# Third layer's attention of a decoder: norms by powers block by block, and its output by batches

## The chip, the cores and the metric

The kernel runs on one core of one Trainium2 chip. A core has five engines, each with an instruction stream of its own: TensorE (PE, matrix products), VectorE (DVE), ScalarE (ACT), GpSimd (POOL) and SyncE (SP), which here only issues DMAs. They wait for each other through semaphores. Transfers run on 16 DMA engines, fed through queues that belong to the issuing engine. The metric is the device time of one execution in microseconds (us). The kernel before takes 1616.43 us, the median of three runs (1613.71 to 1619.91).

## What is computed

A decoder of four layers, each with an attention, a cross attention and a feed-forward part, over 4 batches of 256 tokens with 256 features, in float32. The change touches the attention of the third layer (the code counts from 0 and calls it `l2a_`):

```python
def _softmax_kernel(x, R):
    n = jnp.sqrt(jnp.sum(x * x, axis=-1, keepdims=True))
    x = x / jnp.maximum(n, 1e-06)
    p = jnp.einsum('...d,ed->...e', x, R)
    feats = jnp.concatenate([jnp.sin(p), jnp.cos(p)], axis=-1)
    return feats / math.sqrt(F)
q = (hidden_states @ Wq.T + bq).reshape(b, s, H, D).transpose(0, 2, 1, 3)
k = (hidden_states @ Wk.T + bk).reshape(b, s, HKV, D).transpose(0, 2, 1, 3)
v = (hidden_states @ Wv.T + bv).reshape(b, s, HKV, D).transpose(0, 2, 1, 3)
q = q * cos + _rotate_half(q) * sin
k = k * cos + _rotate_half(k) * sin
k = jnp.repeat(k, rep, axis=1)
v = jnp.repeat(v, rep, axis=1)
qp = _softmax_kernel(q, rand_matrix)
kp = _softmax_kernel(k, rand_matrix)
kv = jnp.einsum('bhsf,bhsd->bsfd', kp, v)
out = jnp.einsum('bhsf,bsfd->bhsd', qp, kv)
out = out.reshape(b, s, HID)
return out @ Wo.T + bo
```

There are 16 query heads and 8 heads of keys and values, of 16 features each. Features are sine and cosine of a random projection of the normalised vector, and the sum over heads is taken for each token by itself. The final reshape goes from (batch, head, token, feature) straight to (batch, row, 256), so it mixes heads and tokens. The input of the stage is a layer norm of the residual, and its output is added to the residual.

## The kernel before

Stages of the decoder run one after the other; every stage is a block of code for each engine, and the next one starts when all engines have ended. `feature_attention` is the stage of the change. Rows of features stand on 128 partitions, the 1024 tokens along the free axis. Keys and values fill one such block (`k0`, `v`), queries two (`q0`, `q1`).

PSUM is used as four pairs of banks of 1024 columns. `Jobs` gives each product in turn the next pair; a list made at the start names the jobs in order and who empties each. `wait_room` makes TensorE wait until the job four places ahead has been emptied, `wait_filled` makes the taker wait for the product.

The front. TensorE projects k, q0, q1, each in two jobs (straight, and with swapped halves for the rotation; the latter's name ends in `s`), then v. VectorE takes each pair of jobs with `rotate` (two operations with cos and sin, one sum) and squares the result. TensorE then forms the squared norms of all three blocks (24 products with 8 columns, `norm`) and the projections by the random matrix (`pk0`, `pq0`, `pq1`). ScalarE takes the root of all norms at once (192 columns), VectorE clamps, inverts and scales them, and makes the turns of each block: product by the inverse norm, a quarter turn for the cosines, and taking away the whole turns. ScalarE applies the sine, TensorE transposes the features back (`fk0`, `fq0`, `fq1`), and ScalarE copies them into `keys` and `q_rows`.

SyncE then makes seven rotated copies each of keys and values, each by two DMAs that shift them by whole heads over the partitions (`rotate_heads`): values first, for all tokens, then keys by halves of the tokens.

The steps. For each half of the tokens there are 8 steps, one for each rotation. VectorE multiplies queries by keys (`by_heads`), TensorE sums over a head's features with a matrix of ones (`weigh`), VectorE multiplies the weights by the values (`mix`), GpSimd adds the results of two steps, and TensorE adds them up in PSUM by transposing them (`add`). The code is written so that `by_heads` of the next step comes before `mix`.

The tail. For each half, ScalarE copies the sums to `att`, SyncE stores four tiles in a scratch of device memory in the order (batch, head, token, feature) and loads them back by rows, TensorE transposes them (`turn_rows`), ScalarE copies, TensorE multiplies by the output matrix (`project_out`) and VectorE adds to the residual. The order of all this is the order in which the code is written for each engine; no scheduler changes it. The layer norm's own inverse root is already made by powers on GpSimd, on 4 columns at a time (`norm_gpsimd`, line 166):

```python
nc.gpsimd.tensor_tensor(m.rstd[:, 1, tiles], m.rstd[:, 0, tiles], m.minus_half[:, tiles], ALU.pow)
```

`m.minus_half` is a small tensor filled with -0.5. In the listing below, lines 2098 to 2100 are the list of jobs, 2133 to 2152 SyncE, 2157 to 2160 GpSimd, 2163 to 2242 TensorE, 2247 to 2273 ScalarE and 2278 to 2339 VectorE.

## Time and profile before

| | |
|---|---|
| median of the runs | 1616.43 us (1613.71 to 1619.91) |
| the profiled execution | 1623.54 us, of which span 1621.7 us |
| busy share of the span: TensorE, VectorE, ScalarE, GpSimd | 70%, 65%, 30%, 35% |
| DMA over the span | 195.87 MB, mean 121 GB/s |
| this stage: first projection to last addition to the residual | 883.16 to 1007.98 us |

The shares are averages over twelve stages with different limits, so they say little on one of them. In the rows, times are counted from the span's start; a row of a timeline may stand for several instructions of one kind, and what stands in brackets is the idle time of the engine before them and what ended it. One product in float32 leaves two records on TensorE, so a job of four 512-column products counts as 8. The granted clock is given in parts of the full 2.4 GHz; 0.50 is the lower of its two levels, 1.2 GHz.

### The profile page before, as it was taken

What the parts mean: (1) busy time and instruction counts of PE and PEld (TensorE: products, weight loads), DVE (VectorE), ACT (ScalarE), POOL (GpSimd) and SP (SyncE); (2) the same over time, 40 slices, a digit from 0 to 9 for tenths busy, and PEclk for the clock granted to TensorE, in tenths of its full rate; (3) what the DMA queues carried; (4) which work ended last, traced back from release to release, by engine and by line L of the source; (5) the groups of instructions that cost most, each with busy time, mean ns of one, the idle gap of its engine ahead of it and who ended that gap; (6) DMA issues with size and microseconds to landing.
All of it is one profiled execution on the core that took longest, in us unless ns stands there. A gap on an engine that the chain in (4) does not pass through costs nothing. (4 is left out here: it accounts for less than half of the span.)

```text
span 1621.7 us, 21361 instructions
## 1 busy us (share of the span) xinstructions
PE 1140.4 (70%) x6058; PEld 718.6 (44%) x6058; DVE 1059.8 (65%) x1790; ACT 492.7 (30%) x949; POOL 575.6 (35%) x596
## 2 busy tenths in 40 slices
PE   7445547999309695554998896699847878866970
PEld 3211235777004572122565644577634324445860
DVE  6999975773695557998885683320345878745454
ACT  3423322333402252332211200343313346622430
POOL 0046613552755113662000042023440632204746
PEclk9769987999659898998999888799978859987985
DMA  5074347996321403433300432142520140048944
GB/s 189 31 255 148 114 137 225 306 315 228 95 68 33 125 4 130 155 130 133 117 1 0 120 77 37 43 144 77 173 85 7 30 129 3 3 125 249 329 137 123
DMA packets 138562, 195.87 MB, mean 121 GB/s; under 512 B 35408, under 2 KB 98914, under 8 KB 137196
## 3 DMA queue, kind: packets, MB, share of 16 engines
q1 hardware_dynamic: 104316, 145.85, 29.0%
q0 software_dynamic: 12704, 29.36, 6.3%
q10 hardware_dynamic: 21456, 19.60, 3.9%
q8 instruction: 43, 0.70, 0.2%
q14 instruction: 43, 0.35, 0.1%
HBM read 142.80 MB, written 31.72 MB: 108 GB/s over the span
## 5 line engine op out<-in xcount | busy, mean ns | idle before, releaser
L165 POOL TENSOR_SCALAR rstd<-moments 128x4 f32<-128x4 f32 x24 | 6.5, 270 | 410.1 <-DVE moments L148 410.1
L177 PE MATMUL psum<-w_ident,h 128*128 128x128 f32 x144 | 29.8, 389 | 110.6 <-DVE h L155 110.6
L558 PE MATMUL psum<-l1s_read,w_ident 128*128 128x512 f32 x128 | 64.9, 630 | 53.5 <-DVE l1s_read L623 53.4
L558 PE MATMUL psum<-l0s_read,w_ident 128*128 128x512 f32 x128 | 65.4, 636 | 52.2 <-DVE l0s_read L623 52.2
L1906 DVE TENSOR_REDUCE l3x_neg<-psum 128x2 f32<-128x512 f32 x128 | 80.7, 683 | 23.9 <-PE psum L1777 23.9
L1881 ACT ACTIVATE l3x_work<-psum 128x512 f32<-128x512 f32 x128 | 72.5, 598 | 50.9 <-PE psum L1800 50.6
L546 POOL TENSOR_TENSOR l1s_drive<-l1s_du,l1s_bc 128x1024 f32<-128x1024 f32 x32 | 75.3, 2355 | 35.3 <-DVE psum L619 35.3
L546 POOL TENSOR_TENSOR l0s_drive<-l0s_du,l0s_bc 128x1024 f32<-128x1024 f32 x32 | 75.2, 2353 | 35.3 <-DVE psum L619 35.3
L177 PEld LDWEIGHTS psum<-w_ident,h 128*128 128x128 f32 x144 | 25.4, 202 | 117.6 <-DVE h L155 115.3
L1162 PE MATMUL psum<-l0f_w_in,l0f_xT 128*128 (+1 forms) x224 | 76.8, 466 | 0.0
L1037 POOL DMA_INDIRECT l3f_x<-l3f_h_rows,l3f_token_of x64 | 59.3, 927 | 48.5 <-DVE l3f_token_of L1433 28.5
L1028 POOL DMA_INDIRECT l0f_x<-l0f_h_rows,l0f_token_now x56 | 59.0, 1053 | 46.6 <-PE psum L1152 18.2
L619 DVE TENSOR_TENSOR_SCAN psum<-psum,l1s_drive 128x1024 f32<-128x1024 f32 x32 | 73.2, 2287 | 0.0
L619 DVE TENSOR_TENSOR_SCAN psum<-psum,l0s_drive 128x1024 f32<-128x1024 f32 x32 | 73.2, 2286 | 0.0
L189 ACT ACTIVATE hT<-psum 128x512 f32<-128x512 f32 x36 | 19.4, 595 | 159.6 <-PE psum L177 159.5
L558 PEld LDWEIGHTS psum<-l1s_read,w_ident 128*128 128x128 f32 x128 | 22.2, 193 | 96.2 <-DVE l1s_read L623 80.3
L558 PEld LDWEIGHTS psum<-l0s_read,w_ident 128*128 128x128 f32 x128 | 22.4, 195 | 95.2 <-DVE l0s_read L623 79.1
L595 ACT ACTIVATE psum<-late,w_l1s_a 128x1024 f32<-128x1024 f32 x32 | 35.7, 1118 | 80.0 <-DVE l1s_read L623 79.4
L595 ACT ACTIVATE psum<-l0s_delta,w_l0s_a 128x1024 f32<-128x1024 f32 x32 | 35.7, 1118 | 80.0 <-DVE l0s_read L623 79.4
L1192 PE MATMUL psum<-l3f_xT,l3f_w_in 128*96 128x96 f32 x528 | 58.0, 255 | 0.3 <-ACT l3f_xT L1293 0.3
L1181 PE MATMUL psum<-l0f_w_down,l0f_gatedT 88*128 (+1 forms) x224 | 57.6, 380 | 0.0
L1192 PEld LDWEIGHTS psum<-l3f_xT,l3f_w_in 128*96 128x96 f32 x528 | 52.3, 171 | 0.6 <-issue 0.5
(642 smaller groups left out, 3131.1 us busy)
## 6 DMA issues: line engine op xcount, KB each, us to landing
l0f_w_in<-in_l0f_w_in SPq DMA_DIRECT2D x56, 352.0 KB
l0s_bc<-l0s_scratch SPq DMA_DIRECT2D x16, 1024.0 KB, 5.1
l1s_bc<-l1s_scratch SPq DMA_DIRECT2D x16, 1024.0 KB, 5.2
l3f_w_in<-in_l3f_w_in SPq DMA_DIRECT2D x32, 384.0 KB
l0f_w_down<-in_l0f_w_down SPq DMA_DIRECT2D x56, 176.0 KB
l2f_w_in<-in_l2f_w_in SPq DMA_DIRECT2D x24, 352.0 KB
l0f_y_rows<-l0f_y ACTq DMA_DIRECT2D x56, 128.0 KB
l3f_w_down<-in_l3f_w_down SPq DMA_DIRECT2D x32, 192.0 KB
```

Of the source, the lines that this page charges most:

```text
L177: ins = nc.tensor.transpose(m.psum[:, at:at + P], m.h[:, t, k * P:(k + 1) * P], m.ident[:])
L546: nc.gpsimd.tensor_tensor(drive[c], du[:, c, :], bc[s][:, 0, :], ALU.mult).then_inc(drive_ready, 1)
L558: ins = nc.tensor.matmul(m.pair(2 + c)[:, cols], lhsT=m.ident[:], rhs=rhs[:, cols], start=start, stop=stop, skip_group_check=True)
L595: nc.scalar.activation(decay[c], delta[:, c, :], ACT.Exp, scale=w["a"][:, c, bass.ds(at, 1)]).then_inc(decay_ready, 1)
L619: nc.vector.tensor_tensor_scan(state[c], decay[c], drive[c], 0.0, ALU.mult, ALU.add).then_inc(scanned, 1)
L1028: nc.gpsimd.indirect_dma_start(x[s][:], None, h_rows, bass.IndirectOffsetOnAxis(ap=token_now[s // 2][:, s % 2:s % 2 + 1], axis=0)).then_in ...
L1037: nc.gpsimd.indirect_dma_start(x[b % ROWS][0:L, :], None, h_rows, bass.IndirectOffsetOnAxis(ap=token_of[0:L, b:b + 1], axis=0)).then_inc(x ...
L1162: ins = nc.tensor.matmul(in_ps[d % 2], lhsT=xT[d % 2][:, k, :], rhs=w, start=(k == 0), stop=(k == KD - 1))
L1181: ins = nc.tensor.matmul(y_ps[d % 2], lhsT=gatedT[d % 2][:, c, :], rhs=w, start=(c == 0), stop=(c == chunks - 1))
L1192: ins = nc.tensor.matmul(feature_ps[i][:, f, :], lhsT=w_in[:, at, k, f * F:(f + 1) * F], rhs=xT[i][:, k, 0:L], start=(k == 0), stop=(k == ...
L1881: nc.scalar.activation(self.prob[i % 8][:, 0:self.keys], self.bank(3 + i % 3)[:, 0:self.keys], ACT.Exp).then_inc(self.exp_done, 1)
L1906: ins = nc.vector.tensor_reduce(self.neg[k % 2][:, :, hl], bank[:, 0:self.keys].rearrange("p (q k) -> p q k", q=self.maxima), AX_X, ALU.ma ...
```

## The change

The norm is now made for each block by itself, as soon as that block is squared. The squared norms of one block are a job of its own (64 columns), emptied by VectorE, which clamps them at 1e-12; GpSimd raises them to the power -0.5 and so gives the inverse norm; VectorE applies it with the factor of the turns in one operation. The square root on ScalarE, the reciprocal and the two scalings are gone. The order on TensorE, VectorE and ScalarE is rewritten so that norms and turns of one block stand between the projections of others. Keys are copied before values, both by halves of the tokens, and each rotation of the values has its own semaphore.

In the tail, work goes by batch in place of halves of the tokens. Sums of a batch are announced as soon as its two tiles are added; stores and loads of batches 0 and 2 go through SyncE's queue, those of 1 and 3 through ScalarE's. Semaphores count accordingly.

```diff
-    jobs = Jobs(m, tag + "in", 2, [(f"{x}{c}{s}", "vector") for x, c in chunks for s in ("", "s")]
-                + [("v", "scalar"), ("norm", "scalar")] + [(f"p{x}{c}", "vector") for x, c in chunks]
-                + [(f"f{x}{c}", "scalar") for x, c in chunks])
+    takers = dict(n="vector", p="vector", f="scalar")
+    order = ["k0", "k0s", "q0", "q0s", "nk0", "pk0", "q1", "q1s", "nq0", "pq0", "fk0", "nq1", "pq1", "v", "fq0", "fq1"]
+    jobs = Jobs(m, tag + "in", 2, [(x, "scalar" if x == "v" else takers.get(x[0], "vector")) for x in order])
...
+
+    def rows_out(eng, b):
+        eng.wait_ge(att_done, b + 1)
+        for t in range(2 * b, 2 * b + 2):
+            dst = scratch[b, :, t % 2 * P:(t % 2 + 1) * P, :].rearrange("h s d -> s h d")
+            eng.dma_start(dst, att[:, t, :].rearrange("p (h d) -> p h d", d=HD)).then_inc(stored[b], 16)
+
+    def rows_back(eng, b):
+        eng.wait_ge(stored[b], 32)
+        eng.dma_start(m.h[:, 2 * b:2 * b + 2, :], by_rows[b]).then_inc(att_back[b], 16)
...
-            sp.wait_ge(jobs.empty("v"), 1)
-            for r in range(1, ROUNDS):
-                rotate_heads(sp, values, r, slice(0, T), values_in)
-            sp.wait_ge(jobs.empty("fk0"), 3)
             for h in range(2):
+                for rows, made, done in ((keys, jobs.empty("fk0"), keys_in), (values, jobs.empty("v"), values_in)):
+                    if h == 0:
+                        sp.wait_ge(made, 1 if rows is keys else 2)
+                    for r in range(1, ROUNDS):
+                        if h:
+                            sp.wait_ge(done[r], 32)
+                        rotate_heads(sp, rows, r, halves[h], done[r])
+            for b in (0, 2):
+                rows_out(sp, b)
+                rows_back(sp, b)
...
+            for i in range(len(chunks)):
+                pool.wait_ge(norm_ready, i + 1)
+                nc.gpsimd.tensor_tensor(norm[:, i, :], norm[:, i, :], m.minus_half[:, 0:1].to_broadcast([P, TILES * HPC]),
+                                        ALU.pow).then_inc(powered, 1)
...
+                for name, lhs, rhs in ((f"n{k}{c}", sq[f"{k}{c}"], w("same")[:, 0:P:HD]), (f"p{k}{c}", x[f"{k}{c}"], w("rand")[:])):
+                    jobs.wait_room(pe, name)
+                    n = rhs.shape[1]
+                    for t in range(TILES):
+                        ins = nc.tensor.matmul(jobs.pair(name)[:, t * n:(t + 1) * n], lhsT=lhs[:, t * P:(t + 1) * P],
+                                               rhs=rhs, start=True, stop=True)
...
+            project_chunk(0)
+            project_chunk(1)
+            norm_and_turns(0)
+            project_chunk(2)
+            norm_and_turns(1)
+            turn_feats(0)
+            norm_and_turns(2)
+            project(m, pe, jobs, "v", wcols(w("v"), 0), hT, KD)
+            turn_feats(1)
+            turn_feats(2)
...
+                    if t % 2:
+                        ins.then_inc(added, 1)
...
+            for h in range(2):
+                for b in (2 * h, 2 * h + 1):
+                    turn_rows(b)
+                if h == 0:
+                    pe.wait_ge(mix_done, STEPS)
+                for b in (2 * h, 2 * h + 1):
+                    project_out(b)
...
+            sine(0)
+            take_feats(0)
+            sine(1)
             jobs.wait_filled(act, "v")
             nc.scalar.activation(values[:, 0, :], jobs.pair("v"), ACT.Identity, bias=w("v_b")[:, 0:1]).then_inc(jobs.empty("v"), 1)
-            jobs.wait_filled(act, "norm")
-            nc.scalar.activation(norm[:].rearrange("p a t h -> p (a t h)"),
+            sine(2)
+            take_feats(1)
+            take_feats(2)
+
+            def take_sums(b):
+                act.wait_ge(added, 2 * (b // 2 + 1) * STEPS // 4 - (1 - b % 2))
...
             take_sums(0)
             take_sums(1)
+            rows_out(act, 1)
+            rows_back(act, 1)
+            take_sums(2)
+            take_sums(3)
+            rows_out(act, 3)
             take_rows(0)
             take_rows(1)
+            rows_back(act, 3)
+            take_rows(2)
+            take_rows(3)
 
...
+            def take_norm(i):
+                k, c = chunks[i]
+                name = f"n{k}{c}"
+                jobs.wait_filled(dve, name)
+                nc.vector.tensor_scalar(norm[:, i, :], jobs.pair(name)[:, 0:TILES * HPC], 1e-12, None, ALU.max).then_inc(norm_ready, 1)
+                dve.wait_ge(norm_ready, i + 1)
+                dve.sem_inc(jobs.empty(name), 1)
+
+            def turns(i, meanwhile=None):
+                k, c = chunks[i]
                 name = f"p{k}{c}"
                 jobs.wait_filled(dve, name)
+                dve.wait_ge(powered, i + 1)
+                r = norm[:, i, :].unsqueeze(2).to_broadcast([P, TILES * HPC, HD])
+                nc.vector.scalar_tensor_tensor(out=heads(f), in0=heads(jobs.pair(name)), scalar=float(1 / TWO_PI), in1=r, op0=ALU.mult,
+                                               op1=ALU.mult).then_inc(jobs.empty(name), 1)
...
+            turn_chunk(0)
+            turn_chunk(1)
+            take_norm(0)
+            turns(0)
+            turn_chunk(2)
+            take_norm(1)
+            o.link(dve, nc.vector.tensor_tensor(m.resid[:], m.resid[:], w("o_b")[:].unsqueeze(1).to_broadcast([P, TILES, D]),
+                                                ALU.add))
+            turns(1, lambda: take_norm(2))
+            turns(2)
...
+            for b in range(B):
+                dve.wait_ge(out_filled, b + 1)
+                r = m.resid[:, 2 * b:2 * b + 2, :]
+                nc.vector.tensor_tensor(r, bank(4 + b).rearrange("p (t d) -> p t d", d=D), r, ALU.add).then_inc(out_added, 1)
+            dve.wait_ge(out_added, B)
```

Three places where instructions move. In the names, `sq` is first the square and then the turns and features of a block, `w_l2a_same` the matrix of ones, `w_l2a_rand` the random matrix; `w_ident` marks transpositions.

TensorE, from the first projection to the last transposition of features, before:

```order
L239 MATMUL psum<-hT,w_l2a_k 128x512 x8
L239 MATMUL psum<-hT,w_l2a_q 128x512 x16
L239 MATMUL psum<-hT,w_l2a_v 128x512 x4
L2178 MATMUL psum<-w_l2a_same,l2a_sq_k 128x8 x8
L2178 MATMUL psum<-w_l2a_same,l2a_sq_q 128x8 x16
L2185 MATMUL psum<-w_l2a_rand,l2a_k 128x128 x8
L2185 MATMUL psum<-w_l2a_rand,l2a_q_rows 128x128 x16
L2193 MATMUL psum<-w_ident,l2a_sq_k 128x128 x8
L2193 MATMUL psum<-w_ident,l2a_sq_q 128x128 x16
```

and now:

```order
L239 MATMUL psum<-hT,w_l2a_k 128x512 x8
L239 MATMUL psum<-hT,w_l2a_q 128x512 x8
L2189 MATMUL psum<-w_l2a_same,l2a_sq_k 128x8 x8
L2189 MATMUL psum<-w_l2a_rand,l2a_k 128x128 x8
L239 MATMUL psum<-hT,w_l2a_q 128x512 x8
L2189 MATMUL psum<-w_l2a_same,l2a_sq_q 128x8 x8
L2189 MATMUL psum<-w_l2a_rand,l2a_q_rows 128x128 x8
L2199 MATMUL psum<-w_ident,l2a_sq_k 128x128 x8
L2189 MATMUL psum<-w_l2a_same,l2a_sq_q 128x8 x8
L2189 MATMUL psum<-w_l2a_rand,l2a_q_rows 128x128 x8
L239 MATMUL psum<-hT,w_l2a_v 128x512 x4
L2199 MATMUL psum<-w_ident,l2a_sq_q 128x128 x16
```

The second q block's projections now stand behind the norms and turns of k, and the values' projection behind all norms; two of the three 8-column groups stand between products of 128 or 512 columns.

VectorE, from the second block's square on, before:

```order
L2287 TENSOR_TENSOR l2a_sq_q<-l2a_q_rows 128x1024
L1556 SCALAR_TENSOR_TENSOR l2a_rot<-psum,w_l2a_q_b,w_l2a_cos 128x1024
L1556 SCALAR_TENSOR_TENSOR l2a_rot<-psum,w_l2a_q_b,w_l2a_sin 128x1024
L1559 TENSOR_TENSOR l2a_q_rows<-l2a_rot 128x1024
L2287 TENSOR_TENSOR l2a_sq_q<-l2a_q_rows 128x1024
L2289 TENSOR_TENSOR resid<-resid,w_l2a_o_b 128x2048
L2293 TENSOR_SCALAR l2a_norm<-l2a_norm 128x192
L2294 RECIPROCAL l2a_norm<-l2a_norm 128x192
L2295 TENSOR_SCALAR l2a_norm<-l2a_norm 128x192
L2302 TENSOR_TENSOR l2a_sq_k<-psum,l2a_norm 128x1024
L2305 TENSOR_SCALAR l2a_sq_k<-l2a_sq_k 128x64x8
L2306 TENSOR_SCALAR l2a_whole<-l2a_sq_k 128x1024
```

and now:

```order
L2324 TENSOR_TENSOR l2a_sq_q<-l2a_q_rows 128x1024
L2330 TENSOR_SCALAR l2a_norm<-psum 128x64
L2342 SCALAR_TENSOR_TENSOR l2a_sq_k<-psum,l2a_norm 128x1024
L2347 TENSOR_SCALAR l2a_sq_k<-l2a_sq_k 128x64x8
L2348 TENSOR_SCALAR l2a_whole<-l2a_sq_k 128x1024
L2349 TENSOR_TENSOR l2a_sq_k<-l2a_sq_k,l2a_whole 128x1024
L1556 SCALAR_TENSOR_TENSOR l2a_rot<-psum,w_l2a_q_b,w_l2a_cos 128x1024
L1556 SCALAR_TENSOR_TENSOR l2a_rot<-psum,w_l2a_q_b,w_l2a_sin 128x1024
L1559 TENSOR_TENSOR l2a_q_rows<-l2a_rot 128x1024
L2324 TENSOR_TENSOR l2a_sq_q<-l2a_q_rows 128x1024
L2330 TENSOR_SCALAR l2a_norm<-psum 128x64
L2358 TENSOR_TENSOR resid<-resid,w_l2a_o_b 128x2048
```

The turns of k stand ahead of the second q block's rotation and behind a clamp and a power; the addition of the bias stands between a clamp and the multiplication that needs its power.

ScalarE, end of the front and the tail, before (it issues no DMA there):

```order
L2258 ACTIVATE l2a_q_rows<-psum 128x1024
L2256 ACTIVATE l2a_sq_q<-l2a_sq_q 128x1024
L2258 ACTIVATE l2a_q_rows<-psum 128x1024
L2262 ACTIVATE l2a_att<-psum 128x1024 x2
L2267 ACTIVATE hT<-psum 128x2x512 x2
```

and now:

```order
L2272 ACTIVATE l2a_sq_q<-l2a_sq_q 128x1024
L2277 ACTIVATE l2a_q_rows<-psum 128x1024 x2
L2290 ACTIVATE l2a_att<-psum 128x512 x2
L2138 DMA l2a_scratch<-l2a_att 128x16x16 x2
L2142 DMA h<-l2a_scratch 128x2x256
L2290 ACTIVATE l2a_att<-psum 128x512 x2
L2138 DMA l2a_scratch<-l2a_att 128x16x16 x2
L2295 ACTIVATE hT<-psum 128x2x256 x2
L2142 DMA h<-l2a_scratch 128x2x256
L2295 ACTIVATE hT<-psum 128x2x256 x2
```

The values' copy, now in front of the last sine, is above the first of these rows. Between the copies of sums and of rows, ScalarE now issues the stores and loads of two batches, and waits for each store before its load.

## Rows read from the trace of the kernel before

**Rows 1.** Timeline of PE, projections: start us, busy us, engine, line, operation.

```profile
890.03 13.90 PE L239 MATMUL psum<-hT,w_l2a_q 128*128 128x512 f32 x32
```

**Rows 2.** Windows: stretch, length, busy us of each engine, PEclk, DMA share, GB/s.

```profile
907.00:934.00 27.00, 20.48 (x121) 19.14 (x119) 15.89 (x18) 10.19 (x10) 0.00 (x0) 0.69 0.72 191
...
944.00:986.00 42.00, 39.55 (x187) 24.46 (x188) 33.35 (x27) 1.53 (x2) 24.25 (x8) 1.00 0.23 30
986.00:1008.30 22.30, 12.49 (x43) 9.55 (x41) 2.45 (x2) 2.45 (x3) 0.00 (x0) 0.77 0.38 47
```

**Rows 3.** Timeline of DVE, front.

```profile
899.75 1.23 DVE L2287 TENSOR_TENSOR l2a_sq_q<-l2a_q_rows 128x1024 f32<-128x1024 f32 x1
900.89 1.28 DVE L1556 SCALAR_TENSOR_TENSOR l2a_rot<-psum,w_l2a_q_b,w_l2a_cos 128x1024 f32<-128x1024 f32 x1
...
907.76 2.28 DVE L2289 TENSOR_TENSOR resid<-resid,w_l2a_o_b 128x2048 f32<-128x2048 f32 x1
915.06 0.26 DVE L2293 TENSOR_SCALAR l2a_norm<-l2a_norm 128x192 f32<-128x192 f32 x1 [5.02 <-ACT l2a_norm L2252]
...
918.31 1.23 DVE L2302 TENSOR_TENSOR l2a_sq_k<-psum,l2a_norm 128x1024 f32<-128x1024 f32 x1 [1.31 <-PE psum L2185]
...
928.17 1.23 DVE L2307 TENSOR_TENSOR l2a_sq_q<-l2a_sq_q,l2a_whole 128x1024 f32<-128x1024 f32 x1
933.74 1.23 DVE L2316 TENSOR_TENSOR l2a_prod<-l2a_q_rows,l2a_keys 128x1024 f32<-128x1024 f32 x1 [4.34 <-ACT l2a_q_rows L2258]
```

**Rows 4.** Timeline of PE, front: norms, turns, transposition.

```profile
907.20 1.85 PE L2178 MATMUL psum<-w_l2a_same,l2a_sq_k 128*128 128x8 f32 x16
...
914.44 3.76 PE L2185 MATMUL psum<-w_l2a_rand,l2a_k 128*128 128x128 f32 x16
917.99 4.97 PE L2185 MATMUL psum<-w_l2a_rand,l2a_q_rows 128*128 128x128 f32 x32
923.22 1.06 PE L2193 MATMUL psum<-w_ident,l2a_sq_k 128*128 128x128 f32 x8 [0.26 <-ACT l2a_sq_k L2256]
```

**Rows 5.** Groups of POOL by form: busy us, mean ns, idle before.

```profile
L546 POOL TENSOR_TENSOR l1s_drive<-l1s_du,l1s_bc 128x1024 f32<-128x1024 f32 x32 | 75.3, 2355 | 35.3 <-DVE psum L619 35.3
...
L166 POOL TENSOR_TENSOR rstd<-rstd,minus_half 128x4 f32<-128x4 f32 x24 | 25.0, 1043 | 2.0
...
L1738 POOL TENSOR_TENSOR l3x_neg_rest<-l3x_neg,l3x_neg_parts 128x16 f32<-128x16 f32 x16 | 3.5, 216 | 1.4
```

**Rows 6.** Instructions on the tile of keys: min/median/max ns, first and last start.

```profile
L2129 SPq DMA_DIRECT2D l2a_keys<-l2a_keys x14: 589/594/611, 925.9 to 942.5; - x14
...
DMA to landing us min/median/max: 2.1/2.4/2.9
```

**Rows 7.** Timeline of PE, begin of the steps.

```profile
935.11 8.34 PE L2201 MATMUL psum<-l2a_prod,w_l2a_same 128*128 128x512 f32 x12 [2.54 <-DVE l2a_prod L2316]
...
948.27 3.60 PE L2201 MATMUL psum<-l2a_prod,w_l2a_same 128*128 128x512 f32 x8
```

**Rows 8.** Timeline of the SP queue, second half's stores and loads.

```profile
986.54 4.03 SPq L2149 DMA_DIRECT2D l2a_scratch<-l2a_att  x4
991.46 3.23 SPq L2152 DMA_DIRECT2D h<-l2a_scratch  x2
```

**Rows 9.** Waits of the SP queue between 994.2 and 996 us.

```profile
SPq L2152 <- DMA l2a_scratch<-l2a_att: 2.2, 1, 2.2
```

**Rows 10.** Timeline of PE, tail.

```profile
987.57 3.69 PE L2228 MATMUL psum<-w_l2a_o,hT 128*128 128x256 f32 x16 [1.25 <-ACT hT L2267]
997.13 1.94 PE L2220 MATMUL psum<-w_ident,h 128*128 128x128 f32 x8 [5.86 <-DMA h<-l2a_scratch]
1000.18 6.53 PE L2228 MATMUL psum<-w_l2a_o,hT 128*128 128x256 f32 x16 [1.11 <-ACT hT L2267]
```

**Rows 11.** Timeline of ACT and of DVE, tail.

```profile
985.49 1.03 ACT L2262 ACTIVATE l2a_att<-psum 128x1024 f32<-128x1024 f32 x1 [19.32 <-PE psum L2210]
...
1006.75 1.23 DVE L2338 TENSOR_TENSOR resid<-psum,resid 128x1024 f32<-128x1024 f32 x1 [14.22 <-PE psum L2228]
```

More of the change, by code:

```diff
@@ L2218, in turn_rows @@
+                                               start=(first == 0 and c == 0 and t % 2 == 0), stop=(first == STEPS // 4 - 1),
+                                               skip_group_check=True)
+                    if t % 2:
+                        ins.then_inc(added, 1)
+            def turn_rows(b):
+                pe.wait_ge(att_back[b], 16)
                 for c in range(KD):
-                    for t in range(4):
-                        ins = nc.tensor.transpose(m.pair(h)[:, c * HALF + t * P:c * HALF + (t + 1) * P],
-                                                  m.h[:, 4 * h + t, c * P:(c + 1) * P], m.ident[:])
+                    for t in range(2):
+                        ins = nc.tensor.transpose(bank(b)[:, c * S + t * P:c * S + (t + 1) * P],
+                                                  m.h[:, 2 * b + t, c * P:(c + 1) * P], m.ident[:])
@@ L2222, in turn_rows, with project_out @@
                 ins.then_inc(rows_turned, 1)
-            def project_out(h):
-                pe.wait_ge(hT_done, h + 1)
-                for t in range(4):
+            def project_out(b):
+                pe.wait_ge(hT_done, b + 1)
+                for t in range(2):
+                    at = (2 * b + t) * P
                     for k in range(KD):
-                        ins = nc.tensor.matmul(m.pair(2 + h)[:, t * D:(t + 1) * D], lhsT=m.hT[:, k, (4 * h + t) * P:(4 * h + t + 1) * P],
+                        ins = nc.tensor.matmul(bank(4 + b)[:, t * D:(t + 1) * D], lhsT=m.hT[:, k, at:at + P],
@@ L2229, in project_out @@
                                                rhs=w("o")[:, k, :], start=(k == 0), stop=(k == KD - 1))
                 ins.then_inc(out_filled, 1)
-            for name in ("fq0", "fq1"):
-                pe.wait_ge(jobs.empty(name), jobs.takers[:jobs.at(name) + 1].count("scalar"))
+            pe.wait_ge(jobs.empty("fq1"), 4)
             for s in range(STEPS):
@@ L2248, in _, with sine, take_feats @@
             m.wait_weights(act, tag)
+            def sine(i):
+                k, c = chunks[i]
+                act.wait_ge(turns_ready, i + 1)
+                nc.scalar.activation(sq[f"{k}{c}"][:], sq[f"{k}{c}"][:], ACT.Sin, scale=SIN_SCALE).then_inc(feats_ready, 1)
+            def take_feats(i):
+                k, c = chunks[i]
+                jobs.wait_filled(act, f"f{k}{c}")
+                nc.scalar.activation(turned_to[f"{k}{c}"], jobs.pair(f"f{k}{c}"), ACT.Copy).then_inc(jobs.empty(f"f{k}{c}"), 1)
@@ L2334, in _ @@
                 mix(s)
-            for h in range(2):
-                dve.wait_ge(out_filled, h + 1)
-                r = m.resid[:, 4 * h:4 * h + 4, :]
-                nc.vector.tensor_tensor(r, m.pair(2 + h).rearrange("p (t d) -> p t d", d=D), r, ALU.add).then_inc(out_added, 1)
-            dve.wait_ge(out_added, 2)
+            for b in range(B):
[3 more added lines that the diff above has]
+            dve.wait_ge(out_added, B)
 def context_mixing(m, n, j):
```

100 lines of the change are left out of this document (27 added, 73 removed).

## Prediction

> **What bounds the kernel now.** I read the page's forty slices to find the third layer's attention, then the windows over its stretch, then the timelines of VectorE, TensorE, ScalarE and the SyncE queue inside it. The stage ends at 1008 us and has a front, sixteen steps and a tail. Up to 907 the projections keep TensorE busy without a gap: 32 matmul records of 512 columns take 13.90 us, so 3.5 us for one job of 8 [rows 1]. From 907 to 934 lies the part of the front that the change rearranges, and nothing is full there: in 27 us TensorE works 20.5, VectorE 15.9, ScalarE 10.2, at a mean granted clock of 0.69 [rows 2]. Then come the steps; in 944 to 986 TensorE is busy 39.6 of 42 us, so they are TensorE's, and the change leaves their instructions as they are [rows 2]. In the tail, 986 to 1008.3, TensorE works 12.5 us and VectorE 2.45 [rows 2]; it waits for round trips through device memory.
>
> In the front VectorE adds the bias from 907.76 on and then waits 5.02 us until 915.06 for one ScalarE square root, behind which all 24 norm groups of TensorE stand. Two more waits follow, 1.31 us before the first multiplication by the norm and 4.34 us before the first step, which starts at 933.74 [rows 3].
>
> **The front after the change.** I walk it from 900.98, where the second square ends (899.75 + 1.23) [rows 3]; up to there all engines have the same work in the same order.
>
> TensorE's own chain, at the full granted clock: a group of norms of 8 columns takes 1.85 us, one of 128 columns 4.97 / 2 = 2.49, a projection job 3.5, a transposition of features 1.06 [rows 1, 4]. The first q block ends at 897.1. Behind it end the norm at 899.0, the turns 901.4, the second q block 908.4, its predecessor's norm 910.3, turns 912.8, features of k 913.9, last norm 915.8, turns 918.3, values 921.8. This chain needs VectorE in time.
>
> The power is the unknown. The trace has powers on 4 columns only, 1043 ns each; an ordinary two-input operation on 16 columns takes 216 ns, on 1024 columns 2355, so 2.1 ns for a column [rows 5]. The new power has 64 columns and is there three times. Lower end: the whole surplus is a fixed cost, 1.04 + 60 x 0.0021 = 1.2 us. Upper end: the surplus of 1.043 - 0.216 = 0.83 us belongs to the 4 columns, 0.207 us each, and 64 x 0.207 + 0.3 = 13.5 us. No row lies between; the only row of a power is sixteen times smaller. I take the geometric mean of the two ends, 4.0 us, and carry both.
>
> With 4.0 us: the clamp of the norm (0.26 us, as at 915.06 for 192 columns) ends at 901.2, its power at 905.2. The turns of one block took 3.7 us (three from 918.31 to 929.40) [rows 3]: k's end at 908.9. The rotation and square of the second q block are two operations of 1.28 and two of 1.23 us, with gaps 5.1: 914.0. Clamp 914.3, power 918.3; the bias add of 2.28 us lies beside it, 1.7 us stay bare. The first multiplication of q0 ends at 919.6, the third clamp at 919.9, its power at 923.9; the other 2.4 us of q0's turns lie beside it, 1.6 us stay bare. Turns of q1: 927.7. From there to the first step come sine, transposition and copy, 4.34 us as now [rows 3]: 932.0. The front wins 1.7 us. Behind VectorE's wait on the first power stands the second q block's rotation, and behind that its norm and turns on TensorE; so each us of power above 4 counts three times. At 1.2 us the walk ends at 927.1, 6.6 us won (then TensorE's 921.8 and the copy of the values in front of the last sine are what is late); at 13.5 us it ends at 960.3, 26.5 lost.
>
> Costed at nothing: the square root and three small VectorE operations leave, but what counts is when the first multiplication starts, and that is in the walk. The two table loads lay in ScalarE's waits. Keys leave earlier, but did not bind: the first step waited for ScalarE [rows 3]. Values now leave behind the keys' first half. 28 copies of keys are issued in 17.1 us, one every 0.63, and land 2.4 us later [rows 6]; so keys go from 915.1 to 924.0 and values to 933.3, the first landing near 928, asked for near 938. Without that cover the price would be the lateness of one pair, under 2 us. The steps run as now with their slow begin, where 12 matmul records take 8.34 us and 8 take 3.60 later [rows 7]. If TensorE's clock stayed up, because its gap before the first step is shorter, 8.3 - 5.4 = 3 us more would be won; I count nothing.
>
> **The tail.** Now the last addition ends at 985.45 and the copy of both batches at 986.5. Four stores are issued from 986.54 to 990.57, the first load at 991.46, the second behind a wait of 2.2 us, its issue ending at 994.69; TensorE starts at 997.13 [rows 8 to 11]. Then 1.94 us of transpositions, a copy, 6.53 us of output matmuls and 1.23 us of VectorE, to 1008.0. The matmuls ran at the lower clock; the first half's took 3.69 us [rows 10].
>
> After the change the additions of batch 2 end 1.0 us before those of batch 3 (half a group, 8 records of 128 columns, 1.06 us [rows 4]) and its copy has half the size, so its stores go at 985.1, those of batch 3 at 986.2 on ScalarE's queue. Bounds: if the queues really ran side by side, the last store would land 4.9 us after its queue's start (991.46 - 986.54), at 991.1, and TensorE could take batch 3 some 2.8 us later, at 993.9, 3.2 us earlier than now. If the DMA engines are the limit, only the earlier start counts, 1.4 us. I take 2.1: 995.0. Then transpositions of half the size (0.5 or 1.0 us), two output groups of half the size (3.69 or 6.53 us together) and an add of 0.65 us, with batch 3's copy beside batch 2's matmuls: 999.9 at the full clock, 1003.2 at half. TensorE's gap before is shorter, since the output of batches 0 and 1 now waits for ScalarE's store issues and ends near 992.4. I take the middle, 1001.5: 6.5 us won (3 to 9 by these bounds).
>
> The Trainium skill, DMA: Bandwidth & Descriptors, section Issuing engines are not separate DMA queues, says that issuing on several engines saves only the sequencer's time. By it the stores end with the engines' work, and the tail would win 5.8 us in place of 6.5. No row of this trace has two queues storing at once.
>
> **Sum.** The profiled execution took 1623.54 us (span 1621.7), 7 us above the median of 1616.43. -1.7 - 6.5 = -8.2: 1615 for a profiled execution, 1608 for the median.
>
> **Rivals.**
> A, the forecast: the power costs between 1.2 and about 5.5 us. The walk gives -6.6 to +2.8 for the front, the tail -6.5: 1603 to 1613, with the tail's own bounds and the clock at the begin of the steps 1599 to 1614. Chance 0.50.
>
> B, slower: the power's cost lies in its columns, 13.5 us. Place: VectorE's wait in front of the second q block, and again before q0's and q1's turns. +26.5 - 6.5 = +20: 1636. Below 4.0 + 8.2 / 3 = 6.7 us for a power the tail pays for the front; from there on it decides. For it: 0.83 us is much for a mere start. Against it: small ordinary operations on GpSimd pay almost only a start [rows 5]. Chance 0.26.
>
> The Trainium skill, GPSIMD Engine Reference, section Instruction dispatch, puts the dispatch of an instruction at tens of cycles and all else into a loop over the elements. That rule makes B right; the trace, with powers of one size alone, cannot say.
>
> C: a power of 5.5 to 9.5 us: -3.7 to +8 in all, 1613 to 1624. Chance 0.12.
>
> D: TensorE's clock falls in the front, since 8-column groups now stand between dense ones. The trace has it at its lower level behind them: 16 records of 128 columns took 3.76 us in place of 2.49, 1.5 times [rows 4]. From the second norm to the values TensorE has 9.8 us of such groups, which become 14.7 by that factor, and 3.5 us of projection, which would double to 7: 8.4 us more. Values 930, the first step near 936, 2 us later than now: 1616.4 + 2 - 6.5 = 1612. Against it: each 8-column group is now only 1.85 us long. Chance 0.06.
>
> E: two queues and smaller pieces win nothing but the earlier start, at the lower clock: -1.7 - 4 = 1611. Chance 0.06.
>
> **How the numbers follow.** Faster or slower means by over 0.5%, 8.1 us, about what a measurement of this kernel can tell from no change. A gives 0.46 faster and 0.04 the same, B 0.26 slower, C 0.10 the same and 0.02 slower, D and E 0.02 faster together (with a power near the lower end) and 0.10 the same: faster 0.48, same 0.24, slower 0.28. Cases of both signs hold weight, so the range takes in B: 1599 to 1637. The forecast's own is 1599 to 1614.
>
> **What would show it.** The three powers of 64 columns on GpSimd: near 4 us each confirms the walk; 1 us puts the first step near 927, 13 us near 960. VectorE's waits in front of the three multiplications by the norm should read 4.0, 1.7 and 1.6 us. TensorE's output matmuls of batches 2 and 3, 3.7 or 6.5 us together, and its start on batch 3's rows, 9.5 us after the last addition in place of 11.7, show the tail. The walk is wrong in itself if a step waits for values or keys, if the second q block does not follow the first turns without a gap on TensorE, or if first step to last addition, 51.7 us now, changes by more than the 3 us of its slow begin.

## The result, and the profile after

| | before | after |
|---|---|---|
| median of the runs, us | 1616.58 | 1634.18 |
| lowest to highest, us | 1613.71 to 1619.91 | 1631.12 to 1637.93 |
| profiled execution, us (span) | 1623.54 (1621.7) | 1632.96 (1631.1) |

The change makes the kernel slower: ratio 1.0101, interval 1.0073 to 1.0128, where 1608 us, a gain, were forecast; 1634 lies inside the wide range of 1599 to 1637, on the side of rival B. The time lies in the three powers. They took 10.52 us each, not 4.0. GpSimd's timeline after (start us, busy us, engine, line, operation, idle before) answers to [rows 5], where powers have 4 columns:

```profile
896.17 10.52 POOL L2164 TENSOR_TENSOR l2a_norm<-l2a_norm,minus_half 128x64 f32<-128x64 f32 x1 [20.17 <-DVE l2a_norm L2330]
915.84 10.52 POOL L2164 TENSOR_TENSOR l2a_norm<-l2a_norm,minus_half 128x64 f32<-128x64 f32 x1 [9.16 <-DVE l2a_norm L2330]
928.06 10.52 POOL L2164 TENSOR_TENSOR l2a_norm<-l2a_norm,minus_half 128x64 f32<-128x64 f32 x1 [1.70 <-DVE l2a_norm L2330]
```

VectorE's timeline of the front, for [rows 3]. The second square ends at 894.73 + 1.22 = 895.95:

```profile
894.73 1.22 DVE L2324 TENSOR_TENSOR l2a_sq_q<-l2a_q_rows 128x1024 f32<-128x1024 f32 x1
895.87 0.22 DVE L2330 TENSOR_SCALAR l2a_norm<-psum 128x64 f32<-128x64 f32 x1
906.80 1.23 DVE L2342 SCALAR_TENSOR_TENSOR l2a_sq_k<-psum,l2a_norm 128x1024 f32<-128x1024 f32 x1 [10.71 <-POOL l2a_norm L2164]
...
915.92 2.36 DVE L2358 TENSOR_TENSOR resid<-resid,w_l2a_o_b 128x2048 f32<-128x2048 f32 x1 [0.16 <-DVE l2a_norm L2330]
926.50 1.23 DVE L2342 SCALAR_TENSOR_TENSOR l2a_sq_q<-psum,l2a_norm 128x1024 f32<-128x1024 f32 x1 [8.22 <-POOL l2a_norm L2164]
...
938.72 1.23 DVE L2342 SCALAR_TENSOR_TENSOR l2a_sq_q<-psum,l2a_norm 128x1024 f32<-128x1024 f32 x1 [8.10 <-POOL l2a_norm L2164]
...
946.73 2.36 DVE L2369 TENSOR_TENSOR l2a_prod<-l2a_q_rows,l2a_keys 128x1024 f32<-128x1024 f32 x2 [4.33 <-ACT l2a_q_rows L2277]
```

Read it as a chain. Each multiplication by the norm (L2342) waits for its own power, and the next power can't start before VectorE has come on: the powers begin at 896.17, 915.84 and 928.06, none beside another. The waits are 10.71, 8.22 and 8.10 us. The sine, transposition and copy before the first step are as before, 4.33 us against 4.34 [rows 3].

TensorE in the front, for [rows 4] (the last row begins the steps, as in [rows 7]):

```profile
894.78 0.83 PE L2189 MATMUL psum<-w_l2a_rand,l2a_k 128*128 128x128 f32 x6
895.45 7.03 PE L239 MATMUL psum<-hT,w_l2a_q 128*128 128x512 f32 x16
902.32 1.85 PE L2189 MATMUL psum<-w_l2a_same,l2a_sq_q 128*128 128x8 f32 x16
908.08 3.78 PE L2189 MATMUL psum<-w_l2a_rand,l2a_q_rows 128*128 128x128 f32 x16 [3.91 <-DVE l2a_sq_k L2342]
...
927.78 6.05 PE L239 MATMUL psum<-hT,w_l2a_v 128*128 128x512 f32 x8 [5.12 <-DVE l2a_sq_q L2342]
...
948.10 8.19 PE L2218 MATMUL psum<-l2a_prod,w_l2a_same 128*128 128x512 f32 x12 [2.53 <-DVE l2a_prod L2369]
```

The first row is the end of the turns of k, since the view begins at 895; the second q block (895.45) follows it without a gap. Then TensorE waits twice for a multiplication that stands behind a power (3.91 and 5.12 us), and the values' 8 records take 6.05 us at a mean granted clock of 0.61, where such a job took 3.5 before [rows 1]. Neither sets the end: VectorE asks for nothing of theirs before its own third power is ready.

The windows cut the stage at the second square's end, the first step, the last addition's end and the last residual addition's end, for [rows 2]:

```profile
895.95:946.73 50.78, 29.00 (x112) 20.64 (x110) 18.66 (x22) 7.24 (x7) 31.55 (x3) 0.73 0.27 79
946.73:997.95 51.22, 47.11 (x194) 26.97 (x195) 40.31 (x32) 1.79 (x3) 25.18 (x8) 0.94 0.40 87
997.95:1013.82 15.87, 12.16 (x48) 9.60 (x46) 2.76 (x4) 2.77 (x5) 0.00 (x0) 0.78 0.54 66
```

Before, the same stretches took 32.8 (900.98 to 933.74 [rows 3]), 51.7 and 22.5 us (985.45 to 1007.98 [rows 11]). So +18.0 in the front, -0.5 in the steps, -6.7 in the tail: +10.8 between these points. In the first window GpSimd's 31.55 us are the powers alone.

The tail after: TensorE (for [rows 10]), then SyncE's queue and ScalarE's (for [rows 8, 9]):

```profile
997.78 1.04 PE L2238 MATMUL psum<-w_ident,h 128*128 128x128 f32 x8
1001.56 6.69 PE L2247 MATMUL psum<-w_l2a_o,hT 128*128 128x256 f32 x16 [2.73 <-ACT hT L2295]
1008.09 1.04 PE L2238 MATMUL psum<-w_ident,h 128*128 128x128 f32 x8
1009.37 3.72 PE L2247 MATMUL psum<-w_l2a_o,hT 128*128 128x256 f32 x16 [0.25 <-ACT hT L2295]
```

```profile
997.71 1.30 SPq L2138 DMA_DIRECT2D l2a_scratch<-l2a_att  x2
1003.93 0.36 SPq L2142 DMA_DIRECT2D h<-l2a_scratch  x1
```

```profile
998.61 2.16 ACTq L2138 DMA_DIRECT2D l2a_scratch<-l2a_att  x2
1000.82 1.08 ACT L2295 ACTIVATE hT<-psum 128x512 f32<-128x512 f32 x2 [2.23 <-issue]
1005.21 0.37 ACTq L2142 DMA_DIRECT2D h<-l2a_scratch  x1
```

From the first store to the start of the last load's issue pass 7.5 us (997.71 to 1005.21). On one queue it was some 7.8: the first store at 986.54, the last load's issue over at 994.69 [rows 8, 9], and one such issue takes 0.36 us. Two queues made the stores hardly faster. TensorE takes up the rows of batches 2 and 3 at 1008.09, 10.1 us after the last addition; before it was 11.7, and 9.5 were forecast. But the output of these batches now follows at once on that of batches 0 and 1 and runs at the full granted clock, 1.00 in place of 0.56: 3.72 us for 6.53 [rows 10]. The other output paid for it: 6.69 us at 0.55 in place of 3.69. It lies beside the round trip, where it costs little: with one queue the last rows were taken up 2.6 us after their load's issue began, which gives 1007.8 here as an estimate, against 1008.09.

### The profile page after: what moved, and what is told of

The parts are those of the page before. It is cut to its first block and busy times, and to the rows that moved or that the text cites. A ratio compares the mean times of both kernels' runs of the same rounds, so it can differ in the third digit from the quotient of the medians.

```text
span 1631.1 us, 21386 instructions
## 1 busy us (share of the span) xinstructions
PE 1140.8 (70%) x6057; PEld 723.9 (44%) x6058; DVE 1059.5 (65%) x1792; ACT 490.3 (30%) x950; POOL 605.4 (37%) x599
## 5 line engine op out<-in xcount | busy, mean ns | idle before, releaser
L546 POOL TENSOR_TENSOR l1s_drive<-l1s_du,l1s_bc 128x1024 f32<-128x1024 f32 x32 | 75.2, 2352 | 35.3 <-DVE psum L619 35.3
L546 POOL TENSOR_TENSOR l0s_drive<-l0s_du,l0s_bc 128x1024 f32<-128x1024 f32 x32 | 75.2, 2352 | 35.3 <-DVE psum L619 35.3
L1881 ACT ACTIVATE l3x_work<-psum 128x512 f32<-128x512 f32 x128 | 72.7, 599 | 50.8 <-PE psum L1800 50.4
L1037 POOL DMA_INDIRECT l3f_x<-l3f_h_rows,l3f_token_of x64 | 59.3, 926 | 50.8 <-DVE l3f_token_of L1433 28.7
L1028 POOL DMA_INDIRECT l0f_x<-l0f_h_rows,l0f_token_now x56 | 58.7, 1049 | 47.0 <-POOL l0f_token_now L1020 17.9
```

The source lines that it names most:

```text
L546: nc.gpsimd.tensor_tensor(drive[c], du[:, c, :], bc[s][:, 0, :], ALU.mult).then_inc(drive_ready, 1)
L1028: nc.gpsimd.indirect_dma_start(x[s][:], None, h_rows, bass.IndirectOffsetOnAxis(ap=token_now[s // 2][:, s % 2:s % 2 + 1], axis=0)).then_in ...
L1037: nc.gpsimd.indirect_dma_start(x[b % ROWS][0:L, :], None, h_rows, bass.IndirectOffsetOnAxis(ap=token_of[0:L, b:b + 1], axis=0)).then_inc(x ...
L1881: nc.scalar.activation(self.prob[i % 8][:, 0:self.keys], self.bank(3 + i % 3)[:, 0:self.keys], ACT.Exp).then_inc(self.exp_done, 1)
```

## The experiments

Theory: the three powers of 10.5 us stand one after another on the path to the first step, and each us of a power counts three times; the tail gives 6 to 7 us back. "Stage" below is the time in a profile from the start of the first power of the layer norm ahead of the attention to that of the next layer norm: 132.8 and 130.4 us in two profiles of before, 143.6 after. The brackets behind a ratio are its 95% interval, the ratio is to the kernel before timed beside it (median 1618 to 1621 us), and a difference in us without a further word is the ratio's.

**The change again.**

> The changed kernel once more, with more rounds. The profile of this stage accounts for 10.9 us of loss (18.0 in the front, -0.5 in the steps, -6.7 in the tail), the timed runs said 17 with an interval from 12 to 21. Theory (the stage is all): 1627 to 1629, ratio 1.007. Rival (something of the change costs 5 us more elsewhere): 1633 or more.

1635.0 us, ratio 1.0103 [1.0080, 1.0127], stage 143.8 and 1487.4 outside it. The slowdown repeats, and the number is the rival's, not the theory's. The stage accounts for 11 to 13 of about 17 us. Outside the stage the profiles of all kernels here lie between 1482.4 and 1492.9 us with no order that I can see, before itself at 1482.4 and 1488.9. So some 3 to 6 us of the slowdown stay unassigned. All other kernels below with the changed order of the front, but the one with half a power, are likewise timed 1 to 6 us slower than their stage says. Whether this is real is not shown.

**Each half alone.** The kernel before with the new output by batches, and the changed front with the old output. Of the first, SyncE's part (the second has the reverse, against the kernel after):

```diff
-            for h in range(2):
-                sp.wait_ge(att_done, h + 1)
...
+            for b in (0, 2):
+                rows_out(sp, b)
+                rows_back(sp, b)
```

> The kernel before with the new tail alone (output by batches, two queues). My theory: the slower time comes from the three powers of the front, and the tail wins. By the trace of the changed kernel the tail from the last addition to the last residual addition is 15.9 us against 22.5, so this kernel is 6.7 us faster than before: 1610. Rival 1 (the tail's gain is given back in the stages behind, or the two queues disturb others): no change, within 2 us. Rival 2 (the tail itself costs): slower.

1612.19 us, ratio 0.9958 [0.9943, 0.9974], -6.8 us, as expected: this half is a gain. From the last addition to the last residual addition pass 15.1 us.

> The changed front (norms by powers, new order, keys before values) with the tail of before. Theory: the front lost 18.0 us from the second square to the first step, all of it in three waits for powers of 10.5 us, so 1616.6 + 17.5 = 1634. Rival (half of the lost time is not in this stage): less than 1628 here, and the rest would show with the changed kernel.

1641.78 us, 1.0151 [1.0131, 1.0171], +24.4; the stage took 151.2, +18.4 to +20.8. Direction right, 7 us more than expected; again some us are outside the stage. The two halves add up: +24.4 - 6.8 = +17.6, against +16.7 for the whole.

**No power.** GpSimd multiplies in place of raising to the power:

```diff
-                                        ALU.pow).then_inc(powered, 1)
+                                        ALU.mult).then_inc(powered, 1)
```

> The changed kernel with a multiplication by -0.5 in place of each power, on the same 64 columns (the features then come from wrongly scaled vectors; all else is the same). Theory: the length of the power is the whole loss. A two-input operation on 64 columns takes about 0.3 us, so VectorE's walk ends about 5 to 6 us ahead of before, the tail wins 6.7, in all 1603 to 1605, with the clock perhaps 3 us more at the begin of the steps. Rival (the new order itself costs: TensorE's low clock behind the 8-column groups, values issued late): 1612 or more.

1605.32 us, 0.9924 [0.9907, 0.9941], some 29 us under after and just above the 1603 to 1605 expected. 26.6 us of the 29 are in the stage (117.1 us). GpSimd, then VectorE with its second rotation, q0's multiplication by the norm and the first step:

```profile
897.08 0.29 POOL L2164 TENSOR_TENSOR l2a_norm<-l2a_norm,minus_half 128x64 f32<-128x64 f32 x1 [20.96 <-DVE l2a_norm L2330]
...
903.50 1.28 DVE L1556 SCALAR_TENSOR_TENSOR l2a_rot<-psum,w_l2a_q_b,w_l2a_sin 128x1024 f32<-128x1024 f32 x1 [1.03 <-PE psum L239]
...
909.99 1.23 DVE L2342 SCALAR_TENSOR_TENSOR l2a_sq_q<-psum,l2a_norm 128x1024 f32<-128x1024 f32 x1
...
921.28 2.36 DVE L2369 TENSOR_TENSOR l2a_prod<-l2a_q_rows,l2a_keys 128x1024 f32<-128x1024 f32 x2 [3.46 <-ACT l2a_q_rows L2277]
```

The second square ends at 896.86 there, so the front takes 24.4 us in place of 32.8. The order of the change is a gain of 8.4 us there; the power alone turns it over. (This kernel leaves the inverse root out and is otherwise the changed one.)

**Half a power.** The power covers 32 of 64 columns:

```diff
-                nc.gpsimd.tensor_tensor(norm[:, i, :], norm[:, i, :], m.minus_half[:, 0:1].to_broadcast([P, TILES * HPC]),
+                nc.gpsimd.tensor_tensor(norm[:, i, 0:32], norm[:, i, 0:32], m.minus_half[:, 0:1].to_broadcast([P, 32]),
```

> The changed kernel with each power on 32 of its 64 columns only (the other norms stay squared; all else is the same). Theory: 0.41 + 32 x 0.158 = 5.5 us for a power, 5.05 less, and all three waits are still bare, so 15 us less than the changed kernel: ratio near 1.001, 1620. Rival (the loss above 4 us does not count three times, because other chains then bind): 1625 or more.

1617.69 us, 0.9981 [0.9961, 1.0001], 2 to 3 us under the expectation.

```profile
902.06 5.42 POOL L2164 TENSOR_TENSOR l2a_norm<-l2a_norm,minus_half 128x32 f32<-128x32 f32 x1 [20.95 <-DVE l2a_norm L2330]
...
937.31 2.36 DVE L2369 TENSOR_TENSOR l2a_prod<-l2a_q_rows,l2a_keys 128x1024 f32<-128x1024 f32 x2 [4.33 <-ACT l2a_q_rows L2277]
```

From 901.85 to 937.31 are 35.5 us. With after's 50.8 the slope is (50.8 - 35.5) / (10.52 - 5.42) = 3.0. To the multiplication's 24.4 us it is (35.5 - 24.4) / (5.42 - 0.29) = 2.2. That follows from the walk too: only the first power is bare from its start. Beside the second lies the bias addition, beside the third the rest of q0's turns, 2.4 us each, and a power shorter than that costs nothing there. With 0.29 us the walk gives 31.0 - 3.7 - 1.7 - 1.6 = 24.0, and in the rows above q0's multiplication indeed waits for nothing. TensorE's own chain shows in one wait of 1.03 us, in front of the second rotation.

**The power by itself,** on seven sizes one after another on an idle GpSimd, in the kernel before:

```diff
+            for cols in (1, 2, 4, 8, 16, 32, 64):
+                half_power = m.minus_half[:, 0:1].to_broadcast([P, cols])
+                m.pool_order.link(pool, nc.gpsimd.tensor_tensor(ladder[:, 64:64 + cols], ladder[:, 0:cols], half_power, ALU.pow))
```

> The kernel before with nine more operations on GpSimd while that is idle in the front, waited for by nobody: a memset, powers -0.5 of 1, 2, 4, 8, 16, 32 and 64 columns and one multiplication of 64 columns. Theory from the two sizes seen (4 columns 1.043 us, 64 columns 10.52): 0.41 us and 0.158 us for each column, so 0.57, 0.73, 1.04, 1.68, 2.9, 5.5, 10.5 us, the multiplication 0.29. Rival (blocks of some columns): steps in it, equal times below the block's size. The time of the kernel stays.

Its groups (busy us, mean ns, idle before); the kernel's one time was 1621.24 us:

```profile
L2161 POOL TENSOR_TENSOR l2a_ladder<-l2a_ladder,minus_half 128x64 f32<-128x64 f32 x1 | 11.3, 11252 | 0.1
...
L2161 POOL TENSOR_TENSOR l2a_ladder<-l2a_ladder,minus_half 128x32 f32<-128x32 f32 x1 | 5.4, 5417 | 0.1
...
L2161 POOL TENSOR_TENSOR l2a_ladder<-l2a_ladder,minus_half 128x16 f32<-128x16 f32 x1 | 2.9, 2895 | 0.1
...
L2161 POOL TENSOR_TENSOR l2a_ladder<-l2a_ladder,minus_half 128x4 f32<-128x4 f32 x1 | 1.0, 1008 | 0.1
...
L2161 POOL TENSOR_TENSOR l2a_ladder<-l2a_ladder,minus_half 128x1 f32<-128x1 f32 x1 | 0.6, 627 | 0.1
L2162 POOL TENSOR_TENSOR l2a_ladder<-l2a_ladder,minus_half 128x64 f32<-128x64 f32 x1 | 0.3, 293 | 0.1
```

(5.417 - 2.895) / 16 = 0.158 us a column, and 5.417 - 32 x 0.158 = 0.37 us is fixed; this gives 1.00 us for 4 columns, measured 1.008, and 0.53 for one, measured 0.627. The front's 10.52 fits it (0.37 + 64 x 0.158 = 10.5); why 64 columns took 11.25 in this run is open.

**The powers, but early.** All norms and powers ahead of the turns (the code of TensorE and VectorE is reordered to match the list):

```diff
-    order = ["k0", "k0s", "q0", "q0s", "nk0", "pk0", "q1", "q1s", "nq0", "pq0", "fk0", "nq1", "pq1", "v", "fq0", "fq1"]
+    order = ["k0", "k0s", "q0", "q0s", "nk0", "q1", "q1s", "nq0", "nq1", "pk0", "pq0", "fk0", "pq1", "v", "fq0", "fq1"]
```

> The changed kernel with the three clamps as early as the squares allow, each block's multiplication behind all three of them: powers run back to back on GpSimd. In the rows of before the chain is 901.2 + 3 x 10.6 = 933, turns of q1 3.7, 4.3 to the first step: 941, against 951.7 with the change as it is, so 10.5 us less than the changed kernel, 1624 to 1625, still 6 more than before. Rival (the loss is in VectorE's and TensorE's order, not in the sum of the powers): within 3 us of the changed kernel.

1622.91 us, 1.0023 [1.0011, 1.0035]. GpSimd:

```profile
897.45 31.49 POOL L2164 TENSOR_TENSOR l2a_norm<-l2a_norm,minus_half 128x64 f32<-128x64 f32 x3 [20.90 <-DVE l2a_norm L2333]
```

The same 31.5 us of powers, now back to back, with VectorE's rotations and turns beside them: some 12 us less than after, still slower than before, as expected. The front takes 39.9 us, 10.9 less than after.

**The root early.** The changed kernel with one ScalarE square root over all three norms ahead of all turns:

```diff
+    order = ["k0", "k0s", "q0", "q0s", "q1", "q1s", "norm", "pk0", "pq0", "pq1", "fk0", "v", "fq0", "fq1"]
...
+            nc.scalar.activation(norm[:].rearrange("p a n -> p (a n)"),
+                                 jobs.pair("norm")[:, 0:len(chunks) * TILES * HPC], ACT.Sqrt).then_inc(jobs.empty("norm"), 1)
```

> No power: one square root on ScalarE for all norms as before, but norms of k and q0 and all turns stand ahead of the values' projection, and k's features ahead of it; keys before values, and the new tail. The walk from before's rows: norms end 909.7 instead of 914.6, square root, clamp and reciprocal to 912.2, three turns of 3.7 us to 923.3, 4.3 us to the first step: 927.6 against 933.7, so 6 us won in front and 6.8 in the tail, 1605 to 1606. Rival (TensorE's chain with the values behind the turns, at the lower clock, sets the end of the front): 4 us less of it, 1609.

1608.93 us, 0.9945 [0.9928, 0.9962], the rival's number. The last group of norms ended 10.5 us behind the second square, not 8.7: its 16 records of 8 columns took 3.58 us at a granted clock of 0.50, and the first group 1.85. And ScalarE shows a table load behind the wait instead of in it:

```profile
906.84 1.28 ACT L2285 ACT_TABLE_LOAD   x1 [27.11 <-PE psum L2184]
908.13 0.33 ACT L2285 ACTIVATE l2a_norm<-psum 128x192 f32<-128x192 f32 x1
```

**One queue for the new tail,** to see what the second queue does:

```diff
-            for b in (0, 2):
-                rows_out(sp, b)
-                rows_back(sp, b)
+            for h in range(2):
+                for step in (rows_out, rows_back):
+                    for b in (2 * h, 2 * h + 1):
+                        step(sp, b)
```

> The new tail alone on the kernel before, with all stores and loads on SyncE's queue (stores of both batches first, then both loads), nothing on ScalarE's. Theory (the stores are bound by the DMA engines; the tail's gain is smaller pieces, earlier start and TensorE at the full clock, not the second queue): same as with two queues within 1 us, 1611 to 1613. Rival (the second queue carries the gain): half of the 6.8 us or less remains, 1615.

1618.44 us, 0.9991 [0.9979, 1.0004]: in the timed runs the gain is nearly gone with one queue, and my expectation fell. The profile says less: from the last addition to the last residual addition 17.5 us, against 22.5 before and 15.1 with two queues, so 5.0 of 7.4 us are there. Where the other 3 us of the timed difference lie is open. Its TensorE:

```profile
986.41 3.69 PE L2237 MATMUL psum<-w_l2a_o,hT 128*128 128x256 f32 x16 [0.39 <-ACT hT L2278]
993.15 0.74 PE L2228 MATMUL psum<-w_ident,h 128*128 128x128 f32 x4 [3.05 <-DMA h<-l2a_scratch]
995.32 1.11 PE L2228 MATMUL psum<-w_ident,h 128*128 128x128 f32 x4 [1.43 <-DMA h<-l2a_scratch]
996.23 5.70 PE L2237 MATMUL psum<-w_l2a_o,hT 128*128 128x256 f32 x16
```

TensorE takes up the last rows 10.2 us after the last addition, hardly later than in the changed kernel with its two queues (10.1). But the first output is early, TensorE then stands still 3 us, and the last output runs at a mean granted clock of 0.63. That gives a new theory: what the second queue buys is clock. It was put to the test by three surplus products in that gap, on one queue still:

```diff
+                if h:
+                    for i in range(3):
+                        nc.tensor.matmul(bank(i % 2), lhsT=m.ident[:], rhs=m.hT[:, 0, 0:HALF], start=True, stop=True)
```

> The tail by batches on one queue, with three surplus products of 512 columns on TensorE (results unused) where it waits for the last batches' rows. In the profile the one-queue tail loses its 2.4 us against two queues by the last output matmuls, 5.7 us at the lower clock in place of 3.7; with two queues ScalarE's store issues happen to push the first batches' output against the last ones'. Theory (TensorE's clock): the last output matmuls take 3.7 us and the kernel gains 2 us over one queue. Rival (the transfers themselves): no gain.

```profile
986.61 2.74 PE L2251 MATMUL psum<-hT,w_ident 128*128 128x512 f32 x6
989.86 0.66 PE L2228 MATMUL psum<-w_ident,h 128*128 128x128 f32 x4 [0.52 <-DMA h<-l2a_scratch]
992.18 0.66 PE L2228 MATMUL psum<-w_ident,h 128*128 128x128 f32 x4 [1.66 <-DMA h<-l2a_scratch]
992.68 3.62 PE L2237 MATMUL psum<-w_l2a_o,hT 128*128 128x256 f32 x16
```

1613.61 us, 0.9959 [0.9942, 0.9977], the ratio of two queues (0.9958). The output took 3.62 us for 5.70, at a granted clock of 1.00, and the stretch from the last addition to the last residual addition 15.2 for 17.5, as with two queues. The stores and loads are as they were (7.8 us from the first store to the last load's issue in both), so the 2.3 us are the clock's. The ratios differ by more, some 5 us.

**The fastest version that keeps the inverse norm.** The early root, its table loaded in the wait by a root of one column, and surplus products around the last transposition:

```diff
+            nc.scalar.activation(first_root[:], m.minus_half[:, 0:1], ACT.Sqrt, scale=-1.0)
...
+            fill(2)
             turn_feats(2)
+            fill(2)
```

> The kernel with one early square root, with two more edits: a square root of one column at the stage's begin, so that the table is loaded before the norms arrive, and two surplus products on TensorE before and behind the last transposition of features, so that it does not idle before the steps. The load stood bare for 1.3 us in the profile of the one without; the first 12 records of the steps took 8.2 us at the lower clock in place of 5.4. Theory: 3 to 4 us less, 1605. Rival (the clock stays down, or the surplus products delay the steps): 1 us less or more time.

1607.69 us, 0.9935 [0.9915, 0.9956]: faster than both kernels, though against the early root alone the intervals overlap. In the profile it is 1.7 us less in the stage, where 3 to 4 were expected. The table load is gone, but it was worth little: with the root 1.3 us earlier, VectorE waits 1.20 us for TensorE's turns of k in place of 0.27, and from the second square to the first step pass 28.4 us for 28.8. The rest comes from the clock, for the steps' first 8 records run at the full one:

```profile
909.38 1.23 DVE L2351 SCALAR_TENSOR_TENSOR l2a_sq_k<-psum,l2a_norm 128x1024 f32<-128x1024 f32 x1 [1.20 <-PE psum L2194]
...
925.30 3.67 PE L2231 MATMUL psum<-l2a_prod,w_l2a_same 128*128 128x512 f32 x8 [0.82 <-DVE l2a_prod L2380]
```

In the early root alone these took 5.21 us, at a mean granted clock of 0.70.

**The kernel before again.**

> The kernel before against itself. It should read the same within 0.25%, and its profile shows how much the other stages vary in themselves: the first profile of it lay 5 us above its median, so all stages but this one should sum to some 1484 us here in place of 1489, while the stage itself should again take 132.8 us between the layer norms' powers.

1619.98 us, 1.0002 [0.9987, 1.0018], stage 130.4 and not 132.8. Small differences between ratios of a few tenths of a per cent are thus at the edge of what was measured. One us of the 2.4 is the last output's, 5.55 us for 6.53 in the same kernel, so a single profile's tail is good to about 1 us.

## Why the prediction was wrong

**The step that failed** is "I take the geometric mean of the two ends, 4.0 us". The power took 10.52 us, inside the bounds of 1.2 and 13.5 but far above the value taken. By the ladder its cost is 0.37 + 0.158 us a column. The upper end was too high mostly because it took the fixed part for that of an ordinary operation, 0.22 us: with 0.37 the same sum gives 0.37 + 64 x 0.168 = 11.1. With two ends so far apart and one row of a single size, 4.0 was a guess; the row of 1043 ns on 4 columns (five times the ordinary operation's 216 [rows 5]) did speak for the columns. So rival B's mechanism is what happened, at a price between B and C. That B's 1636 us is so near the measured 1634 is in part luck: its powers are 3 us too dear, 9 us in the sum, and most of that is made up by what the stage does not explain.

**The walk was right.** Put 10.52 into it and the front comes to -1.7 + 3 x 6.52 = +17.9; measured +18.0. At 5.42 it gives 31.0 + 3 x 1.42 = 35.3 us from the second square to the first step; measured 35.5. The waits grew as it says: 10.7, 8.2 and 8.1 are the forecast's 4.0, 1.7 and 1.6 plus 6.7, 6.5 and 6.5. That the power alone turns the change from a gain into a loss is shown by the multiplication, half a power and the powers back to back. The Trainium skill, GPSIMD Engine Reference, section Instruction dispatch, puts the dispatch at tens of cycles and the work into a loop over the elements. The trace agrees as to the loop: 10.1 us of 10.5 grow with the columns. No run here shows how many cycles the fixed 0.37 us are.

**The tail was right in size and partly wrong in reason.** -6.5 forecast, -6.7 measured in the profile, -6.8 for the tail alone. The stores gain no more than 0.3 us by the second queue (7.5 for 7.8), and TensorE took up the rows 10.1 us after the last addition, not 9.5. That agrees with the Trainium skill, DMA: Bandwidth & Descriptors, section Issuing engines are not separate DMA queues, by which only the sequencer's time is saved, and with the first half of rival E; I had credited more. The output matmuls came to 3.72 us, where I had put the middle of 3.7 and 6.5. I had noted the shorter gap before them, but gave it half its weight. So two errors cancelled, 0.6 us later at the rows and 0.8 us quicker behind them, and that the sum came out is luck. The pair with one queue, with and without surplus products, shows that this clock is what the second queue brings: about 2 us in the profile, some 5 in the timed runs.

**The steps were right.** They wait for neither keys nor values, and their slow begin stays: 8.19 us for 12 records, 8.34 before [rows 7]. Rival D did not decide: the values did run at a low clock (0.61), but beside the powers. The second q block followed the first turns on TensorE without a gap, as the walk wants; the gap of 3.91 us is in front of q0's turns, and it too stood beside a power. One reading of the TensorE chain was wrong: 2.49 us for a group of 128 columns is not at the full clock. The granted clock over 918 to 923 us was 0.74, and in the changed kernel such a group takes 2.03 us. The chain was shorter than I had it, and nothing in the sum hung on it.

**The whole.** The forecast's own sum with the measured power gives +17.9 - 6.5 = +11 us. The stage's profiles say +11 to +13, the timed runs +12 to +21, with 17 in the middle. What makes up the rest is open.

## What to carry to other kernels

Before a function that is known from a few columns goes onto the critical path, time it at its real size; if it can't be timed, treat its surplus over an ordinary operation as growing with the columns. Count how often it stands in series: a split into three that are each waited for pays the length three times. Putting the same three powers together and early gave back only 10.9 us, since they still took 31.5; one square root for all three parts on ScalarE took 0.33 us and stood on the path once. Where a dense block follows a wait, look at what TensorE does in the wait: here surplus products there raised the clock of the block and were worth 2.3 us in the profile, as much as the second queue.
